# Two message-passing layers on one core: every tenth tile of edges becomes a small one whose rows SyncE and ScalarE fetch one by one

## What is computed

```python
# layer 0
x_t  = mlp2(x, W1n, b1n, W2n, b2n)              # a table of 12,500 rows of 64 floats
e_t  = mlp2(edge_attr, W1e, b1e, W2e, b2e)      # one row per edge
out  = x + segment_sum(x_t[src] * e_t * dp_scale, dst) * res_w
x    = layernorm(x + layernorm_affine(out, gamma, beta))
# layer 1
xw   = einsum('ni,rio->rno', x, einsum('rb,bio->rio', w_comp, weight))
x    = layernorm(x + relu(segment_sum(xw[edge_type, src] * edge_weight, dst) + h_bias))
```

## Time and profile before

| | |
|---|---|
| median of 3 runs | 4044.78 us (4036.95 to 4045.75) |
| profiled execution | 4037.32 us, its span on the core 4035.5 us |
| busy: PE, DVE, ACT, POOL | 2582, 2050, 514, 2976 us |
| indirect DMAs | 3128 (1564 a layer) |

### The profile page before, as it was taken

The page is one execution under the profiler, slowest core; times in us unless marked ns, Lnnn a source line. Parts: engine busy times, 40 slices in busy tenths (PEclk is TensorE's granted clock), DMA queues, the critical chain, the costliest instruction groups (busy, mean ns, idle before and its releaser), DMA issues.

```text
span 4035.5 us, 58860 instructions
## 1 busy us (share of the span) xinstructions
PE 2582.1 (64%) x14343; PEld 2213.5 (55%) x14344; DVE 2049.8 (51%) x3777; ACT 514.4 (13%) x1256; POOL 2976.4 (74%) x3191
## 2 busy tenths in 40 slices
PE   7667666767666666666656566666566556666665
PEld 6555555555555555555445555555555555555554
DVE  5333334343443444445455555565656666666566
ACT  3111112121222222222210000000000000000000
POOL 3777777777777777777757777777777777777775
PEclk9777777777777777778777777777777777777877
DMA  4222222222221222222212222222222222222221
GB/s 87 41 40 40 40 40 42 40 42 40 44 44 37 42 42 42 42 42 48 39 28 28 28 28 28 28 30 28 30 28 30 30 30 30 30 30 30 30 30 29
DMA packets 506007, 147.38 MB, mean 37 GB/s; under 512 B 403200, under 2 KB 455668, under 8 KB 505978
## 3 DMA queue, kind: packets, MB, share of 16 engines
q0 software_dynamic: 100096, 102.60, 14.4%
q1 hardware_dynamic: 405882, 44.44, 8.0%
HBM read 137.18 MB, written 9.62 MB: 36 GB/s over the span
## 4 chain that ended last, share of the span: by engine, by line
POOL 55%; issue 22%; DVE 8%; PE 8%; DVEq 3%; DMA 2%; ACT 1%; POOLq 1%; SPq 0%; ACTq 0%
POOL rows L498 55%; PE ps_fin L1166 2%; DMA rows<-node_table,src_ix 1%; DVEq L726 1%; PE ps_agg L1094 1%; PE ps_agg L1088 1%; DVE work L959 1%; PE ps_o L1079 1%; PE ps_o L1020 1%; DVE work L759 1%; PE ps_z L1067 1%; DMA src_ix<-in_src_dram 1%; DVE work L873 1%; DVE norm_stats L870 1%; DVE work L872 1%
## 5 line engine op out<-in xcount | busy, mean ns | idle before, releaser
L498 POOL DMA_INDIRECT rows<-node_table,src_ix x3128 | 2955.0, 945 | 986.1 <-issue 943.6
L1094 PE MATMUL ps_agg<-work 128*128 128x128 f32 x6256 | 1102.9, 349 | 746.3 <-DVE work L959 743.5
L1094 PEld LDWEIGHTS ps_agg<-work 128*128 128x128 f32 x6256 | 1016.4, 255 | 831.5 <-DVE work L959 829.7
L959 DVE TENSOR_TENSOR work<-rows,ps_z 128x1024 f32<-128x1024 f32 x391 | 476.2, 1218 | 535.3 <-DMA rows<-node_table,src_ix 534.6
L759 DVE TENSOR_TENSOR work<-ps_x,rel 128x512 f32<-128x512 f32 x782 | 540.9, 692 | 378.8 <-DVE acc L773 262.5
L1088 PE MATMUL ps_agg<-work 128*64 128x128 f32 x3128 | 570.1, 342 | 12.8 <-issue 12.4
L1088 PEld LDWEIGHTS ps_agg<-work 128*64 128x64 f32 x3128 | 454.5, 175 | 104.6 <-issue 102.7
L1075 PE MATMUL ps_o<-b2e,ones 3*128 3x256 bf16 x391 | 121.3, 310 | 605.7 <-DVE hid L808 604.8
L815 DVE TENSOR_TENSOR work<-ps_o,rows 128x256 f32<-128x256 f32 x391 | 165.0, 422 | 589.7 <-DMA rows<-node_table,src_ix 586.4
L1075 PEld LDWEIGHTS ps_o<-b2e,ones 3*128 3x128 bf16 x391 | 36.3, 93 | 717.6 <-DVE hid L808 709.0
L773 DVE TENSOR_TENSOR acc<-acc,ps_agg 64x128 f32 (+1 forms) x782 | 270.1, 345 | 191.9 <-PE ps_agg L1094 97.2
(11 more groups left out here) (102 smaller groups left out, 1055.0 us busy)
## 6 DMA issues: line engine op xcount, KB each, us to landing
rows<-node_table,src_ix POOLq DMA_INDIRECT x3128, 2.4
attr<-in_edge_attr_dram SPq DMA_DIRECT2D x78, 320.0 KB
node_table<-x_sb SPq DMA_DIRECT2D x14, 224.0 KB, 2.5
node_table<-work SPq DMA_DIRECT2D x24, 128.0 KB, 2.0
out_dram<-x_sb SPq DMA_DIRECT2D x13, 224.0 KB
src_ix<-in_src_dram SPq DMA_DIRECT2D x156, 10.0 KB, 2.0
dst_ix<-in_dst_dram SPq DMA_DIRECT2D x156, 10.0 KB, 2.5
attr<-in_edge_type_dram SPq DMA_DIRECT2D x78, 10.0 KB, 2.4
```

Of the source, the lines that this page charges most:

```text
L498: nc.gpsimd.indirect_dma_start(rows[0:n, slot_of(u), j, :], None, table, bass.IndirectOffsetOnAxis(ap=src_ix[0:n, half_of(u), col : col + ...
L959: nc.vector.tensor_tensor(scaled[:, ring, :, :, :], rows[:, slot_of(u), :, :].rearrange("p j (o f) -> p j o f", o=1).to_broadcast([P, J, B ...
L1094: last = nc.tensor.matmul(bank[:, pr * P : (pr + 1) * P], scaled[:, ring, j, 2 * pr : 2 * pr + 2, :].rearrange("p b f -> p (b f)"), hot[:, ...
```

## The change

Every tenth tile of a body becomes a small one, the "lone" tile, of 152 edges: 76 partitions by 2 columns (`LONE_J`). A body is 9 x 512 + 152 = 4760 edges, so a layer has 42 bodies and a last tile of 80 edges in one column. POOL gathers the nine whole tiles of a body only: 42 x 36 + 1 = 1513 indirect DMAs a layer. The 152 rows of the lone tile are fetched one by one with plain DMAs of one row of 256 bytes, whose address comes from a register: 89 by SP, 63 by ACT. The source indices stand in a new line `lone_ix` in SBUF; SP reads up to 24 of them into registers at a time (batches of 24, 24, 24 and 17), ACT nine at a time.

SP issues its rows in two parts: 48 at the end of the loop's body, when the lone tile before has been multiplied (there is one slot for it), behind the loads of half 1 and behind `next_chunk`; and 41 behind the loads of half 0. ACT issues nine rows after each of the tiles 1 to 7 of a body in layer 0, and all 63 in one go in layer 1. DVE waits for four semaphores ahead of the lone tile. Half 1 now has one small DMA more for each kind of edge data except the source. One-hot, scaling and sums of the lone tile cover 2 columns in place of 4. The spans of targets are found in another arrangement of the indices, in the prologue.

```diff
+    WHOLE = BODY - 1
+    LONE_J = 2
+    LONE_SP, LONE_ACT = 89, 63
...
+        SP_PARTS = ((0, 48), (48, LONE_SP))
+        ACT_FROM, ACT_STEPS = 1, 7
...
+        def fetch_row(engine, l, r, reg, landed):
+            engine.dma_start(
+                rows[r // LONE_J : r // LONE_J + 1, WHOLE, r % LONE_J, :],
+                (node_table, node_table2)[l][bass.ds(engine.snap(reg, min_val=0, max_val=N - 1), 1), :],
+            ).then_inc(landed, 16)
...
+            def load_lone_ix(l, i):
+                sp.dma_start(lone_ix[:], lone_row(src)[bass.ds(i, 1), :]).then_inc(lone_ix_loaded[l], 16)
+
+            def fetch_rows(l, k):
+                for at in range(SP_PARTS[k][0], SP_PARTS[k][1], len(lone_regs)):
+                    regs = lone_regs[0 : min(len(lone_regs), SP_PARTS[k][1] - at)]
+                    sp.reg_load(regs, lone_ix[0:1, at : at + len(regs)])
+                    for r, reg in enumerate(regs):
+                        fetch_row(sp, l, at + r, reg, lone_by_sp[l][k])
...
                 with sp.Fori(0, BODIES - 1) as i:
-                    for h in range(2):
-
-                        sp.wait_ge(msg_ready[l], i * BODY + (h + 1) * GROUP)
-                        load_group(l, h, i * 2 + (2 + h))
+                    sp.wait_ge(msg_ready[l], i * BODY + GROUP)
+                    load_group(l, 0, i + 1)
+                    fetch_rows(l, 1)
+
+                    sp.wait_ge(lone_ix_read[l], i + 1)
+                    load_lone_ix(l, i + 1)
+                    sp.wait_ge(msg_ready[l], i * BODY + BODY)
+                    load_group(l, 1, i + 1)
                     next_chunk(sp, done, limit, i + 1, lambda c: store_chunk(l, c))
+                    sp.wait_ge(lone_ix_loaded[l], i * 16 + 32)
+                    sp.sem_inc(lone_begun[0], 1)
+                    fetch_rows(l, 0)
...
-                for u in range(BODY):
+                for u in range(WHOLE):
                     gather(l, 0, u)
...
+            def fetch_rows(l, i, step):
+                if step == 0:
+                    act.wait_ge(lone_ix_loaded[l], i * 16 + 16)
+                    act.wait_ge(msg_ready[l], i * BODY + ACT_FROM)
+                    act.sem_inc(lone_begun[1], 1)
+                at = LONE_SP + step * ACT_EACH
+                act.reg_load(lone_regs, lone_ix[0:1, at : at + ACT_EACH])
+                for r, reg in enumerate(lone_regs):
+                    fetch_row(act, l, at + r, reg, lone_by_act[l][step >= ACT_PARTS[0]])
+                if step == ACT_STEPS - 1:
+                    act.sem_inc(lone_ix_read[l], 1)
...
+            def rows_landed(l, i, u):
+                if whole(u):
+                    tail_only = isinstance(i, int) and i * BODY + u == FULL
+                    dve.wait_ge(gathered[l][slot_of(u)], FULL_GATHERS if tail_only else uses(i, u) * ALL_GATHERS)
+                else:
+                    for k in range(2):
+                        dve.wait_ge(lone_by_sp[l][k], uses(i, u) * 16 * (SP_PARTS[k][1] - SP_PARTS[k][0]))
+                        dve.wait_ge(lone_by_act[l][k], uses(i, u) * 16 * ACT_EACH * ACT_PARTS[k])
```

More of the change, by code:

```diff
@@ L390, in load_tail @@
                 else:
-                    sp.dma_start(etype[0:TAIL_P, 0, 0:J], rest(edge_type)).then_inc(type_loaded[0], 16)
-                    sp.dma_start(enorm[0:TAIL_P, 0, 0:J], rest(weight_flat)).then_inc(norm_loaded[0], 16)
+                    sp.dma_start(etype[0:TAIL_P, 0, 0:1], rest(edge_type)).then_inc(type_loaded[0], 16)
+                    sp.dma_start(enorm[0:TAIL_P, 0, 0:1], rest(weight_flat)).then_inc(norm_loaded[0], 16)
+            lone_regs = [sp.alloc_register(f"sp_lone{k}") for k in range(24)]
@@ L461, in _ @@
             nc.gpsimd.memset(ones_3[:], 1.0).then_inc(s_pool, 1)
+            nc.gpsimd.memset(dst_ix[:, 1, WHOLES[1] * J :], -(1 << 20)).then_inc(s_lone, 1)
+            nc.gpsimd.memset(rows[:, WHOLE, :, :], 0.0).then_inc(s_lone, 1)
+            nc.gpsimd.memset(attr[:, 1, WHOLES[1], :], 0.0).then_inc(s_lone, 1)
             nc.gpsimd.memset(acc[0:F, 0, 0:ZERO_CUT], 0.0).then_inc(s_pool, 1)
@@ L485, in _, with gather @@
             stage(PAIRS - 1, 0)
-            def gather(l, i, u, slot_used=None, n=P):
+            def gather(l, i, u, slot_used=None, n=P, columns=J):
                 table = (node_table, node_table2)[l]
@@ L495, in gather @@
                 pool.sem_inc(gathers_begun, 1)
-                for j in range(J):
+                for j in range(columns):
                     col = (u % GROUP) * J + j
@@ L506, in _ @@
                 pool.wait_ge(ready, count)
-                for u in range(BODY):
+                for u in range(WHOLE):
                     gather(l, 0, u)
                 with pool.Fori(1, BODIES) as i:
-                    for u in range(BODY):
+                    for u in range(WHOLE):
                         gather(l, i, u, i * BODY + (u + 1 - BODY))
-                gather(l, BODIES, 0, FULL + 1 - BODY, n=TAIL_P)
+                gather(l, BODIES, 0, FULL + 1 - BODY, n=TAIL_P, columns=1)
         @block.scalar
@@ L554, in edge_lower @@
                 ).then_inc(low_ready, 1)
+            lone_regs = [act.alloc_register(f"act_lone{k}") for k in range(ACT_EACH)]
+            def fetch_rows(l, i, step):
[9 more added lines that the diff above has]
+                    act.sem_inc(lone_ix_read[l], 1)
             def step(i, u, last=TILES):
@@ L623, in _ @@
             act.reg_mov(copied, 0)
+            act.wait_ge(table2_ready, 16 * CHUNKS)
             with act.Fori(0, BODIES - 1) as i:
+                for step_u in range(ACT_STEPS):
+                    fetch_rows(1, i, step_u)
                 next_chunk(act, copied, limit, i + 1, lambda c: finish1(c, i * BODY + BODY))
+            for step_u in range(ACT_STEPS):
+                fetch_rows(1, BODIES - 1, step_u)
             remaining_chunks(act, copied, limit, lambda c: finish1(c, TILES))
@@ L1092, in sum_by_target @@
                 for pr in range(2):
-                    for j in range(J):
+                    for j in range(n):
                         last = nc.tensor.matmul(
```

215 lines of the change are left out of this document (136 added, 79 removed).

## The result

The changed kernel takes 5664.3 us (median of 4 runs, 5662.3 to 5665.4) where the kernel before takes 4044.7 (4037.0 to 4045.8): 1.400 times the time, 95% interval 1.3987 to 1.4021. The forecast was 5195 us with a range of 4250 to 5900: the sign and the mechanism came true, and the sum was 469 us short. The profiled execution has a span of 5661.6 us.

A forecast was written before the change was run, and what follows sets the result against it. POOL's own gather issuing was taken to bound the kernel before, and SP's row issuing with the store's wait after. 128 + 42 x (51.2 + 53.0) + 689 + 2 = 5195 us, range 4250 to 5900.

The forecast's parts named there:

- One row on SP: Address and issue of one single-row DMA on SP: 0.45 us, bounds 0.33 and 0.56; 89 rows 40.1 us.
- rivals 1 and 2: POOL stays the bound, 3910 us, 15%; or cheaper rows of about 0.35 us with flat reads, about 4220 us, 11%.
- rival 3: Index reads in proportion to registers, 6500 us; with everything over 5750, also SP's and ACT's issues hindering each other, 8%.
- The reads: SP's reads of 24 indices into registers: 1.0 us each, four a cycle 3.8 us (1.1 to 19.3).
- flat: A read on SP costing the same for 24 registers as for one, 0.28 us; -227 us on the sum.
- the step of 0.215 us: Extra time on DVE for two registers over one; in proportion, a read of 24 would take 5.2 us.
- The rest of the cycle: SP's half loads, question and handover beside rows and reads; cycle sums 51.2 us in layer 0, 53.0 in layer 1.
- question and semaphore: SP's question after a chunk, with some six register and branch instructions: 0.9 us together, an estimate.
- handover: Lone tile's passing from SP's rows to DVE: landing 1.6 us, multiplication 0.3, two semaphores 0.2; 2.1 us.
- The waits ahead of the rows: SP's stop in `store_chunk` ahead of 48 rows, 13 times a layer: 32 and 21 us each, 689 us in all.
- Head, gap and tail: Time before, between and after the layers' gathers: 80.6 + 24.7 + 22.6, 128 us in the sum.
- ACT: ACT's row steps of 4.8 us, nine-index reads 0.5; 45 us a body in layer 0, 32 in layer 1, hidden.

The follow-up runs named there:

- No rows on SP: Changed kernel with rows 0 to 88 of each lone tile left out, ACT keeping its 63; 4833.6 us beside 4045.2 for the kernel before.
- store late with one read: Changed kernel with the chunk's store and its wait behind the 48 rows, and SP's registers read once per cycle; 4946.2 us beside 4037.3 before.
- twelve tiles: Changed kernel with groups of six tiles, 80-edge lone tile, 35 bodies, 48 SP and 32 ACT rows, store behind rows; 4023.4 us, 0.9963 of before.

## Why the prediction was right, and where its sum was short

*The bound and its move.* Right: POOL's own issuing bounded the kernel, 102 gathers fewer freed 127 us, and SP's cycle took the bound over. No rows on SP, store late with one read, and twelve tiles show it from three sides: take SP's work away and POOL or ACT sets the pace; give SP fewer rows and a longer cycle, and the gathers follow one another again without waiting for their indices.

*One row on SP.* 0.45 us forecast. The 48 and 41 rows less the two reads inside are 22.06 + 18.90 - 3.25 = 37.7 us for 89, 0.424 each; the issue is 0.228 us, the rest address and gaps. The value was 6% high and the lower bound of 0.33 held, so rivals 1 and 2 fell by it. On ACT a row takes 0.377, with SP's rows beside it and without them (no rows on SP), so SP's issues don't hinder ACT's, against that part of rival 3.

*The reads.* 1.0 us forecast for 24, 1.63 measured (the median); the four of a cycle take 6.2 us in place of 3.8. 1.63 us is 68 ns a register, between flat and the step of 0.215 us that the earlier trace rows show from one register to two, so rival 3 fell too. The Trainium skill, Runtime: NRT & Kernel Launch, section "Instruction fetch mechanics", whose 200 ns a register would have made 4.8 us of it (an estimate from that figure), disagrees with this trace for reads from SBUF; no run here read from HBM. Rows and reads together are 44.2 us in place of 43.9: the two errors cancelled, and that was luck.

*The rest of the cycle.* Here the sum was short by omission. In layer 1: loads of both halves 5.4 us (forecast 6.1), question and semaphore 1.3 (0.9), handover 1.6 (2.1), and 0.6 for `lone_ix` and a gap, which I had left out. What the sum put at nothing is SP's waiting for its own instructions: the gap of 2.80 us at the loop's branch, and in layer 0 the second one behind it (4.6 in all at that place). Cycles of 56.1 in place of 51.2 and 53.0 are 42 x (4.9 + 3.1) = 336 us of the 469, and these gaps alone, 274 us, are the largest term that was left out.

*The waits ahead of the rows.* Right in kind and number. With 36.1 and 26.6 us a chunk in place of 32 and 21 they were mis-sized by 13 x 4.1 + 13 x 5.6 = 126 us. In layer 1 I had let the tiles run faster up to the chunk and shorten the wait; it did not shorten (25.4 us against 26.2). In layer 0 I had started from a mean that the short wait behind the loop pulls down. And the store itself, with what stands beside it, adds 1.2 us to each wait.

*Head, gap and tail.* 128 us taken over from before; 80.9 + 44.4 + 48.6 = 174 measured: 46 us. These three come to 508, 39 too many: 84 full cycles with 26 chunks would make 5527 us, and the two layers last 5488. The first and last cycles of a layer lack a part each; I have not followed them singly.

*ACT.* Forecast at 45 us a body in layer 0, hidden behind SP. It was hidden, but only by 4 us: its reads of nine took 2.14 us, not 0.5, over even the 2.0 that I had as their upper end, a step 6.0, not 4.8, and the body 51.6 where ACT alone bounds it (no rows on SP). Had SP's terms been right, ACT's would have set layer 0. Its stand in a layer-1 chunk, with rows behind, I had not seen at all.

## What to carry to other kernels

Work moved off the engine that bounds a kernel costs what it costs on the engine that takes it, per item and per cycle, and it inherits every wait that stands ahead of it there: here 89 issues of 0.42 us on SP and 63 on ACT replaced 1.2 gathers of 1.25 us in each body (102 in 84 bodies). Before moving it, lay the receiving engine's whole cycle out, with branch, reads and handover, against the cycle of the old bound, and ask which engine comes second. Move no more than the slack holds, and put it ahead of the waits that it does not depend on. Look for gaps that no semaphore ends, and for the traffic of the instruction queue in them, before calling such a gap a wait for data. And count the ends: a shorter loop gains only what head, gap and tail don't give back.

## What the runs showed of the hardware

Reads into registers were very uneven. Nine registers took 2.0 to 2.2 us on ACT from six starting indices (89, 98, 107, 125, 134, 143; medians in the changed kernel) and 1.01 us from the seventh, 116, the only one that is a multiple of four. Eight registers from multiples of eight took 0.72 us. On SP 24 registers took 1.43, 1.68 and 1.63 us from the indices 0, 24 and 48, and 17 from 72 took 1.46. That the start's alignment is the cause on ACT is my reading; no run varied it alone.

A loop on SP that holds 89 unrolled rows paid 2.4 us at its branch in each round, and in layer 0 another 1.8 behind it, with one packet of instructions in each gap and 432 packets in the run in place of 17. With 48 rows to a round q14 still moved 357 packets, but the branch took 0.21 us. At which size the gap begins was not tried.

The two kinds of issues ran beside the gathers without slowing them: a gather is busy for 944 to 946 ns with no single rows beside it, with 5600 and with 12,768.
